# One local convolution over 16 samples in 512-column matmuls instead of two over 8 samples in 256-column ones

## The reference

```python
x = x + _L0_conv_ref(_gn(x), ...)
x = x + _L1_conv_ref(_gn(x), ...)
x = x + _L2_conv_ref(_gn(x), ...)   # here: _gn, and inside: out + lepe
x = x + _L3_conv_ref(_gn(x), ...)

# in _L2_conv_ref
lepe = lax.conv_general_dilated(vimg, lepe_w, (1, 1), 'SAME', feature_group_count=c)
out = out + lepe.transpose(0, 2, 3, 1).reshape(b, n, c)
```

## Time and profile before

| | |
|---|---|
| median of 3 runs | 3348.86 us (3343.7 to 3350.99) |
| the profiled execution, its own time | 3347.6 us |
| its span in the trace | 3345.7 us |
| the block of `local_part` in it | from 1386.6 to 1711.6 us |

### The profile page before, as it was taken

One profiled execution on the slowest core, in us unless ns is written; L12 is line 12 of the kernel. 1 busy time (PEld: TensorE's weight loads), 2 busy tenths in 40 slices (PEclk: granted clock), 3 DMA queues, 4 the chain that ended last, 5 costly groups with the idle time before them and its releaser, 6 DMA issues. The chain is left out here.

```text
span 3345.7 us, 71291 instructions
## 1 busy us (share of the span) xinstructions
PE 2799.6 (84%) x25684; PEld 2506.2 (75%) x25684; DVE 2159.8 (65%) x5052; ACT 1368.2 (41%) x2113; POOL 251.6 (8%) x633
## 2 busy tenths in 40 slices
PE   5777769999999999536768887884999999999891
PEld 3566659999999999512336666663999999999791
DVE  6777746666666666763116777776666666666864
ACT  3666642246632222243335555553223664222120
POOL 1001010000000000142100100101000000000502
PEclk9888879999999999757879999997999999999795
DMA  4333230000000000373036566564300000000669
GB/s 84 76 80 89 69 115 0 0 0 0 0 0 0 0 0 0 103 200 88 13 56 85 83 91 100 78 93 65 53 0 0 0 0 0 0 0 0 103 97 144
DMA packets 745180, 164.55 MB, mean 49 GB/s; under 512 B 738801, under 2 KB 739441, under 8 KB 740209
## 3 DMA queue, kind: packets, MB, share of 16 engines
q1 hardware_dynamic: 676736, 151.29, 23.8%
q10 hardware_dynamic: 68336, 11.72, 2.1%
HBM read 95.87 MB, written 67.11 MB: 49 GB/s over the span
## 5 line engine op out<-in xcount | busy, mean ns | idle before, releaser
L280 PE MATMUL L_conv<-L_x_hi,L_w_hi 128*128 128x256 f32 x5040 | 1250.9, 283 | 71.0 <-DVE L_w_lo L246 40.0
L280 PE MATMUL L_conv<-L_x_hi,L_w_lo 128*128 128x256 f32 x5040 | 1249.3, 283 | 0.0
L280 PEld LDWEIGHTS L_conv<-L_x_hi,L_w_hi 128*128 128x128 f32 x5040 | 958.7, 190 | 74.1 <-issue 40.2
L165 ACT ACTIVATE L_row_b<-S,L_bias 128x256 f32 (+1 forms) x1008 | 513.9, 510 | 1177.6 <-DVE L_x_hi L219 1156.1
L280 PEld LDWEIGHTS L_conv<-L_x_hi,L_w_lo 128*128 128x128 f32 x5040 | 957.0, 190 | 0.0
L229 DVE SCALAR_TENSOR_TENSOR S<-L_conv,L_neg_bias,L_row_b 128x256 f32 x1008 | 487.4, 484 | 510.3 <-PE L_conv L284 509.0
L284 PE MATMUL L_conv<-L_x_lo,L_w_hi 128*128 128x256 f32 x5040 | 770.6, 284 | 5.5 <-DVE L_x_lo L221 5.5
L284 PEld LDWEIGHTS L_conv<-L_x_lo,L_w_hi 128*128 128x128 f32 x5040 | 677.3, 190 | 7.7 <-DVE L_x_lo L221 7.7
L221 DVE TENSOR_TENSOR L_x_lo<-S,L_x_hi 128x256 fp32r<-128x256 f32 x1016 | 452.8, 446 | 34.7
L219 DVE TENSOR_SCALAR L_x_hi<-S 128x256 fp32r (+1 forms) x1016 | 318.3, 313 | 35.3
L611 PE MATMUL dc_conv<-dc_xz_hi,dc_w_hi 128*128 128x512 f32 x384 | 176.7, 460 | 96.9 <-DVE dc_w_lo L729 96.9
(11 more groups left out here) (178 smaller groups left out, 2932.5 us busy)
## 6 DMA issues: line engine op xcount, KB each, us to landing
dc_raw<-x SPq DMA_DIRECT2D x32, 512.0 KB, 6.5
x_scratch<-dc_raw SPq DMA_DIRECT2D x16, 1024.0 KB, 7.4
lp_xr<-x_scratch SPq DMA_DIRECT2D x16, 1024.0 KB, 5.9
x_scratch<-lp_xr SPq DMA_DIRECT2D x32, 512.0 KB, 5.9
at_G<-x_scratch SPq DMA_DIRECT2D x64, 256.0 KB, 6.5
at_res<-x_scratch SPq DMA_DIRECT2D x32, 512.0 KB, 6.8
x_scratch<-at_res SPq DMA_DIRECT2D x64, 256.0 KB, 5.2
fs_buf<-x_scratch SPq DMA_DIRECT2D x32, 512.0 KB, 6.1
```

The costliest lines, as they stand in the source:

```text
L165: nc.scalar.activation(row_b[p][:, :, :], line(k, at_step(k, i), p), ACT.Identity, bias=bias[:, k:k + 1]).then_inc(row_b_ready[p], 1)
L280: nc.tensor.matmul(out, w[:, k, s * P:(s + 1) * P], x_hi[p][:, s:s + J, :], start=(s == 0 and n == 0), stop=False)
```

## The change

The convolution runs once, over all 16 samples: 64 taps with 512 (and 496) columns in place of 128 with 256 (and 248). It starts when all 16 samples are normalised. `group` and `normalise` of samples 8 to 15 follow those of samples 0 to 7 directly. Six PSUM banks are cycled in place of four.

```diff
 RING = 4
+BANKS = 6
...
-    taps = [ctx.enter_context(nc.psum_tensor(f"lp_taps{u}", [P, 512], F32)) for u in range(4)]
+    taps = [ctx.enter_context(nc.psum_tensor(f"lp_taps{u}", [P, 512], F32)) for u in range(BANKS)]
...
-    def column(part, blocks, w, p):
-        return S[...][part, blocks, w, p * NB:(p + 1) * NB]
+    def column(part, blocks, w):
+        return S[...][part, blocks, w, :]
...
-            for n in range(NB):
+            for n in range(B):
                 normalise(n)
             act.wait_ge(consts_in, 2 * 16)
             for w in range(W):
-                keep(0, w)
-                if w % 8 == 7:
-                    normalise(NB + w // 8)
-            for w in range(W):
-                keep(1, w)
+                keep(w)
...
-            def taps_of(p, w):
-                g = p * W + w
-                if g >= 4:
-                    pe.wait_ge(taps_kept, g - 3)
-                out = taps[g % 4][:, 0:J * NB].rearrange("p (i b) -> p i b", b=NB)
+            def taps_of(w):
+                if w >= BANKS:
+                    pe.wait_ge(taps_kept, w - BANKS + 1)
+                out = taps[w % BANKS][:, :].rearrange("p (i b) -> p i b", b=B)
...
-            for n in range(NB):
+            for n in range(B):
                 group(n)
             pe.wait_ge(bands.loaded, 8 * 16)
-            pe.wait_ge(normed, NB)
-            for w in range(W):
-                taps_of(0, w)
-                if w % 8 == 7:
-                    group(NB + w // 8)
             pe.wait_ge(normed, B)
             for w in range(W):
-                taps_of(1, w)
+                taps_of(w)
```

More of the change, by code:

```diff
@@ L864, in local_part @@
     dve_step, pool_step = sem("dve_step"), sem("pool_step")
-    def column(part, blocks, w, p):
-        return S[:, 2:2 * BLOCKS, :, :].rearrange("p (a q) j b -> p a (q j) b", q=2)[part, blocks, w, p * NB:(p + 1) * NB]
+    def column(part, blocks, w):
+        return S[:, 2:2 * BLOCKS, :, :].rearrange("p (a q) j b -> p a (q j) b", q=2)[part, blocks, w, :]
     lo, hi, every = slice(0, HALF), slice(HALF, P), slice(0, P)
@@ L906, in normalise, with keep @@
                                      bias=affine[:, n, 1:2], scale=affine[:, n, 0:1]).then_inc(normed, 1)
-            def keep(p, w):
-                g = p * W + w
-                act.wait_ge(taps_done, g + 1)
-                nc.scalar.activation(column(every, slice(0, J), w, p), taps[g % 4][:, 0:J * NB].rearrange("p (i b) -> p i b", b=NB),
+            def keep(w):
+                act.wait_ge(taps_done, w + 1)
+                nc.scalar.activation(column(every, slice(0, J), w), taps[w % BANKS][:, :].rearrange("p (i b) -> p i b", b=B),
                                      ACT.Identity, bias=lb[:, w:w + 1]).then_inc(taps_kept, 1)
@@ L930, in group @@
                 nc.tensor.matmul(group_ps[:, 2 * n:2 * n + 2], avg[:, :], me[:, n, :], start=True, stop=True).then_inc(group_done, 1)
-            def taps_of(p, w):
-                g = p * W + w
-                if g >= 4:
-                    pe.wait_ge(taps_kept, g - 3)
-                out = taps[g % 4][:, 0:J * NB].rearrange("p (i b) -> p i b", b=NB)
-                nc.tensor.matmul(out, bands.band0[:, w, :], column(every, slice(0, J), w, p), start=True, stop=False)
-                nc.tensor.matmul(out[lo, 1:J, :], bands.band1[hi, w, :], column(hi, slice(0, J - 1), w, p), start=False, stop=True)
-                nc.tensor.matmul(out[hi, 0:J - 1, :], bands.band1[lo, w, :], column(lo, slice(1, J), w, p),
+            def taps_of(w):
+                if w >= BANKS:
+                    pe.wait_ge(taps_kept, w - BANKS + 1)
+                out = taps[w % BANKS][:, :].rearrange("p (i b) -> p i b", b=B)
+                nc.tensor.matmul(out, bands.band0[:, w, :], column(every, slice(0, J), w), start=True, stop=False)
+                nc.tensor.matmul(out[lo, 1:J, :], bands.band1[hi, w, :], column(hi, slice(0, J - 1), w), start=False, stop=True)
+                nc.tensor.matmul(out[hi, 0:J - 1, :], bands.band1[lo, w, :], column(lo, slice(1, J), w),
                                  start=False, stop=True).then_inc(taps_done, 1)
             pe.wait_ge(consts_in, 2 * 16)
-            for n in range(NB):
+            for n in range(B):
                 group(n)
             pe.wait_ge(bands.loaded, 8 * 16)
-            pe.wait_ge(normed, NB)
-            for w in range(W):
-                taps_of(0, w)
-                if w % 8 == 7:
-                    group(NB + w // 8)
             pe.wait_ge(normed, B)
             for w in range(W):
-                taps_of(1, w)
+                taps_of(w)
         @block.vector
```

## The result

The changed kernel takes 3306.25 us (median of 4 runs, 3304.28 to 3310.21) against 3349.93 us of the kernel before (4 runs, 3343.7 to 3358.6). The ratio is 0.9875, with an interval from 0.9855 to 0.9894, which is some 42 us (35 to 49) of the kernel before: small, but clear of 1. The forecast was 3310 with a range of 3303 to 3319. The profiled execution took 3304.28 us for a span of 3302.4, 43.3 less than the span before.

A forecast was written before the change was run, and what follows sets the result against it. The prediction took a ring of waits to bound the kernel's block. Taps from 1539.05, plus 129.9, 2.8, 0.13 and 0.69, end it at 1672.6, 39.0 us earlier: 3348.86 - 39.0 = 3310 us, range 3303 to 3319.

The forecast's parts named there:

- The ring of waits: Pass 0 beside samples 8 to 15: VectorE, ScalarE and TensorE wait on each other in turn, 19.62 us a sample.
- second stretch: Part of the old block with pass 0 of the taps beside samples 8 to 15: 159.3 us, no engine near full.
- Rival (e): Whole block: the change does nothing, since something else hid the ring of waits; chance 0.01.
- The time before the taps: Normalisation of all samples: seven more at 8.10 us, then 18.95 us to the chain's end; taps start at 1539.05.
- Rival (d): Normalisation: samples 9 to 15 come slower than 8.10 us as DMA nears its end; 3320 us at 9.5; chance 0.04.
- A tap: Convolution on TensorE: one 512-column tap takes 2.03 us at full clock, 64 of them 129.9 us.
- (a): Taps: weight loads vanish behind the longer matmuls, a tap takes 1.67 us, 3287 us in all; chance 0.06.
- (b): Taps grow by more than their columns, to 2.17 to 2.39 us; 3319 to 3333 us in all; chance 0.07.
- The clock at the start: First taps on TensorE: 5.9 us at the lower clock lose 2.8 us, bounds 1.7 and 6.
- Rival (c): Taps: TensorE at 512 columns with six banks does not hold the upper clock; 3423 us; chance 0.02.
- The keeps: ScalarE's writes out of PSUM: 0.69 us each, hidden behind taps; only the last counts, starting 0.13 us after its tap.
- The sum: Block end: all terms give 1672.6 against 1711.6 before, 39.0 us less; nothing given back elsewhere; 3310 us.

The follow-up runs named there:

- order-only kernel: Kernel before with all 16 samples normalised ahead of the taps, still two passes of 256 columns and four banks: 3323.34 us, ratio 0.9927.
- skewed order: Kernel before, taps still beside the normalisation, with `group` matmuls two samples further ahead and six banks: 3273.28 us, ratio 0.978.

## Why the prediction was right, and where it was not

**The ring of waits** was the bound of the second stretch, as read from the earlier trace rows. The order-only kernel, the six banks in the old order and the skewed order each moved the block as the ring says: by 25.4, 27.2 and 79 us. Rival (e) is out.

**The time before the taps** holds the one step that failed: "In the earlier trace rows the sum of sample 8 starts at 1463.42." It is sample 9's, and the earlier trace rows are of samples 5 to 9, not 4 to 8 as their line says. The sums must be counted from that of sample 0: in the new trace sample 9's starts at 1457.99 - 1381.21 = 76.8 us after the block's start, and the row taken for sample 8 at 1463.42 - 1386.6 = 76.8. So there were six samples to go, not seven: one period, 8.1 us, too much. With it out, the first tap is forecast at 1530.95 - 1386.6 = 144.3 after the block's start; measured, 144.3. The pace of 8.10 us held (8.09), and so did the end of the chain (18.95 forecast, 19.07 measured). Rival (d) is out.

**A tap**: 2.03 forecast, 2.033 measured; its price at the lower clock 3.84 forecast, 3.82 measured. The shortest record is 592 ns, that of L1335 590. What stays out of the doubling was put at 0.36 us a tap, 23 us in all; measured it is 2.033 - 2 x 0.831 = 0.37, and the width is worth 21.0 to 22.3 us by the order-only kernel. What this remainder consists of no run takes apart. Rivals (a) and (b) are out. The Trainium skill's rule ("TensorE: Matmul & The Clock Gate", section Back-to-back issue gap), which with four passes gave 1.70 us, an estimate, stays 0.33 us a tap too low here. The rule of the same page's section Step-by-step, that the next tile's weights load during this tile's matmul, is not what these taps show: the remainder stayed although the matmuls doubled, and the load of a tap's first weights (PEld, 1655.67) is recorded from the same moment as its matmul, 0.07 us before the matmul ahead of it ends (1655.16 + 0.58).

**The clock at the start**: forecast 5.9 us at 0.50 and 2.8 us lost. The window shows 0.50 for 4.0 us and 1.00 behind it. The first two taps took 1531.54 - 1525.54 = 6.0 us in place of 4.07, so 1.9 us were lost, 0.9 less. (The bound of 6 us above follows from no row: the 8.8 us of the earlier trace rows would lose 4.1 at this price.) Rival (c) is out: TensorE's clock was 1.00 over the 129 us of the rest. The swing of the clock that the Trainium skill describes for banks cycled at 512 columns, there in bf16 (same page, section A second HAM failure mode: psum-queue depth-cycling), did not occur in these float32 taps: 1.00 over 129 us with six banks and with four, and over 100 us with one.

**The keeps**: 0.69 us, hidden, the last one 2.16 us after the start of the last tap (2.03 + 0.13). Six banks or four decide nothing, as said. The prediction's "with fewer than two banks it would be paid" came true with one bank: 53.8 us.

**The sum.** The forecast of the block's gain was 39.0 us and the trace has 47.7: 8.1 of the difference is the miscount, 0.9 the clock at the start, and -0.3 the rest. That the median was only 4 us below the forecast, not 9, is luck: in both pairs of traces the other stages gave some 4 us back (4.4 and 4.2), which the prediction had put at nothing and no run explains. With the block's 47.7 us alone the median would have been near 3348.86 - 47.7 = 3301.2, below the range; the range of 3303 to 3319 held the time, near its lower end, because one error covered part of the other. "The attention as long as before" is right within a wandering of 10 us, and so could not have been told from one pair of traces.

## What to carry to other kernels

Where no engine is near full over a stretch, follow one item through the waits: if the small step that lets the next item start is queued behind work that waits for this item, the cure is to issue that step ahead, before giving up the overlap. Taking the overlap out cost nothing here because the ring had already cost more; with the ring opened instead, the same overlap was worth 31 us more than the change. And when a time is carried on from a repeated row, count the repetitions from the first one, with its own start beside it.

## What the runs showed of the hardware

Stages with the same code wandered by 7 to 10 us between the eleven traces, while the block itself repeated within 1 us (277.3 and 277.4, 325.0 and 325.8). The stretch with one bank kept the granted clock at 1.00 although every tap was preceded by 0.79 us without a matmul:

```profile
1540.00:1640.00 100.00, 72.50 (x208) 16.79 (x208) 0.00 (x0) 24.03 (x35) 0.00 (x0) 1.00 0.00 0
```

Widths of 7 and 9 samples, in runs of 28 and 36 bytes at a stride of 4 KB, cost TensorE next to nothing beyond their columns. The taps of all four widths fit one line, a fixed part and the 0.831 us for each 256 columns that the earlier trace rows give: 1.09 us at 224 columns, 1.193 at 256, 1.31 at 288 and 2.033 at 512 leave 0.36, 0.36, 0.38 and 0.37. That makes 0.36 to 0.38 us the price of one more tap of three float32 matmuls at each of these widths.
